# The last 128 tokens of a transformer block's result computed by tokens instead of by channels, with residual and gate brought to that layout by small copies on chip

## The reference, cut to what matters

```
x = x + causal_depthwise_conv(x, cond)          # x: 32 batches x 32 steps x 256 channels
# transformer block, conditioned by cond through six vectors per batch
shift1, scale1, gate1, shift2, scale2, gate2 = split(cond @ ada_w + ada_b, 6)
x1   = ln(x) * (1 + scale1) + shift1
attn = softmax(q k^T / sqrt(128)) v, 16 heads, over the 32 steps of a batch
xa   = x + gate1 * (attn @ out_w + out_b)
x2   = ln(xa) * (1 + scale2) + shift2
h    = gelu(x2 @ ffn_w1 + ffn_b1)               # 1024 hidden values per token
out  = x + xa + gate2 * (h @ ffn_w2 + ffn_b2)   # 1024 tokens x 256 channels
```

## Time and profile before

| | |
|---|---|
| median of 3 runs | 304.48 us (304.09 to 304.7) |
| the profiled execution | 304.34 us, its span 302.5 us |
| TensorE busy | 295.8 us (98% of the span) |
| VectorE busy | 183.0 us (60%) |
| ScalarE, GpSimd busy | 171.4 us (57%), 121.8 us (40%) |
| granted TensorE clock, mean | 0.996 |

### The profile page before, as it was taken

The page is one execution under the profiler, slowest core; times in us unless marked ns, Lnnn a source line. Parts: engine busy times, 40 slices in busy tenths (PEclk is TensorE's granted clock), DMA queues, the critical chain, the costliest instruction groups (busy, mean ns, idle before and its releaser), DMA issues.

```text
span 302.5 us, 6172 instructions
## 1 busy us (share of the span) xinstructions
PE 295.8 (98%) x2598; PEld 250.0 (83%) x2598; DVE 183.0 (60%) x323; ACT 171.4 (57%) x310; POOL 121.8 (40%) x104
## 2 busy tenths in 40 slices
PE   7999999999999999999999999999999999999994
PEld 7896898878898888788888888888888888877884
DVE  3997697997867648472446664350721364859533
ACT  5953377534862765485267736644763695624910
POOL 5207839331811553172337134630916381321410
PEclk9999999999999999999999999999999999999998
DMA  7912422400250061007003400520090000000404
GB/s 227 367 41 71 119 91 70 142 0 2 62 217 0 4 210 71 0 2 277 3 2 111 168 0 2 177 103 0 4 339 8 2 0 3 0 1 2 69 0 69
DMA packets 22427, 23.00 MB, mean 76 GB/s; under 512 B 9240, under 2 KB 15488, under 8 KB 22400
## 3 DMA queue, kind: packets, MB, share of 16 engines
q1 hardware_dynamic: 20720, 22.39, 22.6%
q10 hardware_dynamic: 1680, 0.23, 0.4%
HBM read 21.57 MB, written 1.05 MB: 75 GB/s over the span
## 4 chain that ended last, share of the span: by engine, by line
PE 85%; DVE 11%; POOL 1%; issue 1%; ACT 0%; DVEq 0%; POOLq 0%
PE bank L1051 16%; PE bank L1052 16%; PE bank L1053 16%; PE bank L1139 8%; DVE xc L591 6%; PE bank L1059 5%; PE bank L1061 5%; PE bank L1060 5%; PE bank L1123 3%; PE bank L1267 3%; PE bank L1269 2%; PE bank L1268 2%; DVE pt L741 1%; DVE ol L746 1%; POOL wl L314 1%; PE bank L1010 1%
## 5 line engine op out<-in xcount | busy, mean ns | idle before, releaser
L314 POOL TENSOR_TENSOR wl<-raw,wh 128x512 fp32r<-128x512 f32 x70 | 96.0, 1396 | 119.2 <-ACT wh L387 100.8
L442 ACT ACTIVATE pool<-bank,bT 128x512 f32<-128x512 f32 x56 | 38.5, 688 | 50.4 <-PE bank L1053 50.4
L1051 PE MATMUL bank<-x1h,wl 128*128 128x512 f32 (+1 forms) x180 | 66.8, 371 | 0.0
L1052 PE MATMUL bank<-x1l,wh 128*128 128x512 f32 (+1 forms) x180 | 65.7, 365 | 0.0
L1053 PE MATMUL bank<-x1h,wh 128*128 128x512 f32 (+1 forms) x180 | 65.6, 365 | 0.0
L746 DVE SCALAR_TENSOR_TENSOR ol<-bank,bT,oh 128x512 fp32r<-128x512 f32 x32 | 23.9, 749 | 31.6 <-ACT oh L467 30.8
L591 DVE SCALAR_TENSOR_TENSOR xc<-x,condT,xc 128x496 f32<-128x496 f32 (+27 forms) x76 | 39.9, 593 | 0.1
L387 ACT ACTIVATE wh<-raw 128x512 fp32r<-128x512 f32 x70 | 39.8, 622 | 0.0
L1051 PEld LDWEIGHTS bank<-x1h,wl 128*128 128x128 f32 x180 | 34.0, 189 | 6.4 <-issue 1.0
L1053 PEld LDWEIGHTS bank<-x1h,wh 128*128 128x128 f32 x180 | 34.0, 189 | 5.5
L1052 PEld LDWEIGHTS bank<-x1l,wh 128*128 128x128 f32 x180 | 34.0, 189 | 5.0
(11 more groups left out here) (136 smaller groups left out, 426.0 us busy)
## 6 DMA issues: line engine op xcount, KB each, us to landing
raw<-in_L_cond_qkv_w_dram SPq DMA_DIRECT2D x24, 512.0 KB, 5.7
raw<-in_L_cond_out_w_dram SPq DMA_DIRECT2D x8, 512.0 KB, 3.6
raw<-in_L_cond_ffn_w_dram SPq DMA_DIRECT2D x3, 512.0 KB, 7.0
adaw<-in_L_cond_ada_w_dram SPq DMA_DIRECT2D x1, 1024.0 KB, 10.3
out_dram<-pool SPq DMA_DIRECT2D x12, 64.0 KB, 1.9
xtok<-in_x_dram SPq DMA_DIRECT2D x2, 256.0 KB, 3.1
adaw<-in_L_cond_ada_w_dram SPq DMA_DIRECT2D x1, 512.0 KB, 5.2
xtok<-in_x_dram SPq DMA_DIRECT2D x1, 512.0 KB, 6.0
```

The source lines that it names most:

```text
L314: g.tensor_tensor(wl[:, cols], raw[:, cols], wh[:, cols].bitcast(F32), ALU.subtract)\
L442: a.activation((q_sb if j < GH else k_sb)[:, j % GH, :], src, ACT.Identity, bias=bias(U, j // GH, j % GH)).then_inc(s_ev, 1)
L1051: pe.matmul(dst, wl[:, w_cols], a_hi, start=start, stop=False)
L1052: pe.matmul(dst, wh[:, w_cols], a_lo, start=False, stop=False)
```

## The change: what it does

Half 1 is split at 384 tokens. Pieces 2 and 3 are `ct` 0 and `ct` 1 with the first 384 tokens each, in the old way. The last 128 tokens are computed for both `ct` at once by `ffn2_last`: the hidden values are stationary, the 256 columns of the second layer's weights move, and the result has one token per partition and all 256 channels in a row. It needs no transpose, and it is stored by two DMAs of 64 tokens each (`store_last`), in runs of 1 KB, one from SyncE and one from ScalarE.

Residual and gate are then wanted by tokens too. `last_rest_by_blocks`, put on VectorE between two `hidden_low`, makes gate * bias + residual for the 128 tokens, and transposes it and the gate in blocks of 32 x 32. Sixteen DMAs from SyncE, from one on-chip tile to another, put these blocks where the token layout has them (32 partitions x 4 runs of 128 bytes each). VectorE ends with a multiply by the gate, from the bank, and an add of the rest.

```
-        FFN2_PIECES = [(0, 0, YB[0][:, ALL], ALL), (0, 1, YB[1][:, ALL], ALL), (1, 0, YB[0][:, ALL], ALL),
-                       (1, 1, YB[1][:, FRONT], FRONT), (1, 1, PB[0][:, FRONT], BACK)]
+        ALL, FRONT, BACK = slice(0, HT), slice(0, HT - P), slice(HT - P, HT)
+        FFN2_PIECES = [(0, 0, YB[0][:, ALL], ALL), (0, 1, YB[1][:, ALL], ALL), (1, 0, YB[0][:, FRONT], FRONT),
+                       (1, 1, YB[1][:, FRONT], FRONT)]
...
+        def store_last(eng, i):
+            rows_i = slice(i * P // 2, (i + 1) * P // 2)
+            eng.dma_start(out[B_LAST:B].rearrange("b t c -> (b t) c")[rows_i], last_rows[rows_i]).then_inc(s_out, 16)
...
             # SyncE, after the stores of half 0
+            sp.wait_ge(s_lturn, 2 * CT)
+            for b in range(QB):
+                for i in range(P // T):
+                    sp.dma_start(pe_[T * b:T * (b + 1), :].rearrange("t (q i c) -> t q i c", i=P // T, c=T)[:, :, i, :],
+                                 last_turned[T * i:T * (i + 1), :, T * b:T * (b + 1)]).then_inc(s_lrows, 16)
+            sp.wait_ge(s_turn, 3)
+            for i in range(P // T):
+                store_blocks(sp, 1, 0, i, FRONT)
+            sp.wait_ge(s_turn, 4)
             for i in range(2):
-                store_blocks(sp, 1, 1, i, BACK)
+                store_blocks(sp, 1, 1, i, FRONT)
+            sp.wait_ge(s_fin, 5)
+            store_last(sp, 0)
...
             # ScalarE
             a.wait_ge(s_turn, 4)
-            for i in range(P // T):
+            for i in range(2, P // T):
                 store_blocks(a, 1, 1, i, FRONT)
-            a.wait_ge(s_turn, 5)
-            for i in range(2, P // T):
-                store_blocks(a, 1, 1, i, BACK)
+            a.wait_ge(s_fin, 5)
+            store_last(a, 1)
...
+            def last_rest_by_blocks():
+                v.wait_ge(s_pt, QB * (NU + 1))
+                for ct in range(CT):
+                    rest = by_batch(part(x0, ct, LAST_SPAN))
+                    v.wait_ge(s_lo, CT * (NC + 1) + ct + 1)
+                    v.wait_ge(s_xs, CT + ct + 1)
+                    v.scalar_tensor_tensor(out=rest, in0=ada(GATE2, ct, LAST_SPAN),
+                                           scalar=bT[:, B_F2 + ct:B_F2 + ct + 1],
+                                           in1=by_batch(part(xc, ct, LAST_SPAN)), op0=ALU.mult, op1=ALU.add)\
+                        .then_inc(s_lbias, 1)
+                    v.wait_ge(s_lbias, ct + 1)
+                    v.transpose(by_batch(last_turned[:, ct, :]), rest).then_inc(s_lturn, 1)
+                    v.transpose(by_batch(last_turned[:, CT + ct, :]), ada(GATE2, ct, LAST_SPAN)).then_inc(s_lturn, 1)
...
             hidden_low(1, 5)
+            last_rest_by_blocks()
             hidden_low(1, 7)
...
-            gated(4)
-            turn(4)
+            v.wait_ge(s_f2, 5)
+            v.wait_ge(s_lrows, 16 * QB * P // T)
+            v.tensor_tensor(last_rows, LAST_BANK, last_gate, ALU.mult).then_inc(s_gt, 1)
+            v.wait_ge(s_gt, 5)
+            v.tensor_tensor(last_rows, last_rows, last_rest, ALU.add).then_inc(s_fin, 1)
...
+            def ffn2_last(k):
+                pe.wait_ge(s_hlo[k % 2], (MT + k) // 2 + 1)
+                # w_hi, w_lo: the 256 columns of k's weights
+                pe.matmul(LAST_BANK, hh[:, k, BACK], w_lo, start=(k == 0), stop=False)
+                pe.matmul(LAST_BANK, hl[:, k, BACK], w_hi, start=False, stop=False)
+                m = pe.matmul(LAST_BANK, hh[:, k, BACK], w_hi, start=False, stop=(k == MT - 1))
+                if k == MT - 1:
+                    m.then_inc(s_f2, 1)
```

More of the change, by code:

```diff
@@ L172, in cond_resid_block_kernel @@
         s_turn = sem("result_blocks_turned")
+        s_lbias, s_lturn = sem("last_rest_with_bias"), sem("last_rest_and_gate_turned")
+        s_lrows = sem("last_rest_and_gate_by_tokens")
         s_out = sem("stored")
@@ L211, in cond_resid_block_kernel @@
         ADA_STEPS = [1, 3, 4]
-        ALL, FRONT, BACK = slice(0, HT), slice(0, HT // 2), slice(HT // 2, HT)
-        FFN2_PIECES = [(0, 0, YB[0][:, ALL], ALL), (0, 1, YB[1][:, ALL], ALL), (1, 0, YB[0][:, ALL], ALL),
-                       (1, 1, YB[1][:, FRONT], FRONT), (1, 1, PB[0][:, FRONT], BACK)]
+        ALL, FRONT, BACK = slice(0, HT), slice(0, HT - P), slice(HT - P, HT)
+        FFN2_PIECES = [(0, 0, YB[0][:, ALL], ALL), (0, 1, YB[1][:, ALL], ALL), (1, 0, YB[0][:, FRONT], FRONT),
+                       (1, 1, YB[1][:, FRONT], FRONT)]
+        LAST_BANK = PB[0][:, 0:C]
+        LAST_SPAN = (TOK - P, P)
+        B_LAST = B - QB
+        last_turned = pn[:, :].rearrange("p (q f) -> p q f", q=2 * CT)
+        last_rest, last_gate, last_rows = pe_[:, 0:C], pe_[:, C:2 * C], sd[:, 0:C]
         x_v = x.rearrange("(n q) t c -> (q t) n c", q=QB)
@@ L284, in _ @@
                     sp.dma_start(dst.rearrange("p (k n) -> p k n", k=4), w2_v[:, 0:4, :]).then_inc(s_raw[i], 16)
-            for n, ct in ((0, 0), (0, 1), (1, 0)):
-                sp.wait_ge(s_turn, CT * n + ct + 1)
+            for ct in range(CT):
+                sp.wait_ge(s_turn, ct + 1)
                 for i in range(P // T):
-                    store_blocks(sp, n, ct, i, ALL)
-            sp.wait_ge(s_turn, 5)
+                    store_blocks(sp, 0, ct, i, ALL)
+            sp.wait_ge(s_lturn, 2 * CT)
[7 more added lines that the diff above has]
+            sp.wait_ge(s_turn, 4)
             for i in range(2):
-                store_blocks(sp, 1, 1, i, BACK)
-            sp.wait_ge(s_out, 16 * (5 * P // T))
+                store_blocks(sp, 1, 1, i, FRONT)
+            sp.wait_ge(s_fin, 5)
+            store_last(sp, 0)
+            sp.wait_ge(s_out, 16 * (4 * P // T + 2))
         @block.gpsimd
@@ L1271, in ffn2 @@
                     m.then_inc(s_f2, 1)
+            def ffn2_last(k):
+                pe.wait_ge(s_hlo[k % 2], (MT + k) // 2 + 1)
+                if k < MT // 2:
+                    c0 = 2048 + C * k
+                    w_hi, w_lo = wh[:, c0:c0 + C], wl[:, c0:c0 + C]
+                else:
+                    i, c0 = (k - 4) // 2, C * (k % 2)
+                    w_hi, w_lo = late_hi[:, i, c0:c0 + C], late_lo[:, i, c0:c0 + C]
+                pe.matmul(LAST_BANK, hh[:, k, BACK], w_lo, start=(k == 0), stop=False)
[3 more added lines that the diff above has]
+                    m.then_inc(s_f2, 1)
             last = NU - 1
@@ L1298, in _ @@
             pe.wait_ge(s_gt, CT)
-            for piece in (2, 3, 4):
+            for piece in (2, 3):
                 for k in range(MT):
                     ffn2(piece, k)
+            for k in range(MT):
+                ffn2_last(k)
 _INS = ['x', 'cond_2048', 'L1_cond_ada_w', 'L1_cond_ada_b', 'L1_cond_qkv_w', 'L1_cond_qkv_b', 'L1_cond_out_w',
```

## The result

The changed kernel takes 307.64 us (median of 5, 307.35 to 308.05), the kernel before 304.09 (5 runs, 304.05 to 304.7): ratio 1.0109, 95% interval 1.0097 to 1.0121. It is slower by 1.1%, where "same" was the likeliest, and its time lies above the range of 303.3 to 305.2. The profiled execution took 308.05 us, the longest of the five, its span 306.3.

What follows compares the result with a forecast made beforehand. SyncE's queue was to bound the end: first copy at 289.33 plus 11.04 of steps gives 300.37, plus 1.6 landing 301.97, 0.17 ahead of before; 304.17 profiled, 304.3 against the median, range 303.3 to 305.2; same 0.49.

Steps and rivals of the forecast that it cites:

- the gain at TensorE's end: After TensorE's last product: VectorE done 0.5 us earlier, both last stores issued 0.87 us ahead if nothing else held.
- rival 2: SyncE's queue at the end: all 21 steps take 0.55, last store starts at 301.24, time 305.2 to 305.5; chance 0.17.
- the wait of VectorE for the copies: Before VectorE's last multiply: sixteenth copy lands at most 0.25 us past TensorE's end, and this wait costs nothing.
- signs of being wrong: Gap before SyncE's last store; copy steps over 0.04 from 0.50; L982 after 298.7; TensorE's last product not ending 298.4 within 0.1.
- TensorE's part: TensorE's pieces 2, 3 and last 24 products: 11.30 us against 11.31 before, last product ending at 298.36 as before.
- When the copies can start: VectorE's six operations before the copies: second scalar_tensor_tensor held by GpSimd to about 288.6, SyncE's first copy issued at 289.33.
- What an issue costs: Per DMA on SyncE's queue: 0.50 us for copies, 0.53 for stores of 48 KB; bounds 0.28 and 0.55.
- the 300.37 of the sum: Start of SyncE's last store: first copy at 289.33 plus 22 steps totalling 11.04 us.
- The landing: SyncE's last store, issue to landing: 1.6 us taken, against 1.7 to 1.9 in the rows, landing at 301.97.
- SyncE's store has 1 us of cover: At the end, SyncE's last store waits for its own queue, so 1 us of VectorE's delay by copies stays hidden.
- The threshold in the text: VectorE's wait for the sixteenth copy costs nothing unless copies land later than 2.7 us after their issue.
- -0.17 predicted: End of the kernel: last store lands at 301.97, 0.17 us ahead of 302.14 in the kernel before.

## Why the prediction was wrong, point by point

The mechanism was right in the main: "the gain at TensorE's end is real and is eaten by a queue". The queue was SyncE's, without a break up to the last store but one, and the slower side of it was in the text as rival 2. Its size was wrong, and with it the wait of VectorE for the copies, which the text had at nothing. All four of the text's signs of being wrong came: steps of 0.645, L982 at 301.32, a gap of 0.42 on SyncE's queue ahead of its last store, and a last product that ends at 298.70.

- *TensorE's part* held. From the first product of piece 2 to the start of the last one it took 11.15 us (287.27 to 298.42), against 11.17 before (286.89 to 298.06). That the last product was 0.36 later is no doing of the change: all of this stretch lay 0.4 later in this execution, with the `hidden_low` ahead of the six at 286.14 instead of 285.75, and the lag was there at 26 us.
- *When the copies can start* held in its mechanism, with the second L959 held up by GpSimd as described; that GpSimd's operation decides was shown by the other order of the six and by the same order at an earlier time. That the number came so near, 289.55 against 289.33, is partly luck: the stretch lay 0.4 later, and from the `hidden_low` ahead to the first copy it was 3.41 where the text had 3.58. The working was wrong in one point: transposes of 128 columns did overlap (0.23 and 0.20 from one start to the next), so the second L959 was ready at 287.56 against GpSimd's 287.55, and not 0.2 behind it.
- *What an issue costs* is the step that failed. I took 0.50 for a copy from stores to device memory, with 0.36 for the step behind the first and 0.55 as the upper bound. It was 0.645, with 0.83 behind the first. Fifteen steps from the first copy to the sixteenth took 299.39 - 289.55 = 9.84 instead of 7.36, and the next, to the first store, 0.645 instead of 0.50. That is 2.6 of the 3.25 us by which the last store was later than the 300.37 of the sum. The rest: 0.22 from the start, 0.37 from the open gap, 0.03 in the stores' own steps, which at 0.54 on average were right. Rows 6 and 7 had no DMA that is on chip at both ends, and I counted the number of partitions as the likeness that mattered. The upper bound of 0.55 was one of another kind of DMA, and so none for this kind.
- *The landing* of the last store, 1.6 taken, was 2.2: 0.6 more. I argued that fewer runs take less time; the bounds of 1.7 to 1.9 that the rows gave were too low too. The store of 128 tokens in the same runs of 1 KB landed in 1.7, so it is not the runs; what it is stays open.
- "SyncE's store has 1 us of cover" was wrong in kind: the copies' slower steps delay VectorE and SyncE together, so VectorE's multiply was 2.6 us late, and with SyncE's last store moved away 2.2 us of loss remained. The threshold in the text, a landing later than 2.7 us after issue, looked at the landing (1.83, near enough) and not at the issue.

Together: -0.17 predicted, + 3.25 for the last store's start, + 0.6 for its landing, is 3.7, and the span grew by 3.7 (302.54 to 306.26). Of this, 0.4 is the later stretch of this execution.

The Trainium skill, "DMA: Bandwidth & Descriptors", section "Issuing engines are not separate DMA queues", says that DMAs from several engines save only the time to start them, which is usually small beside the DMA itself. The second part doesn't fit here: one issue of 0.645 is a third of the 1.8 that a copy takes to land, and sixteen in a row took 10 us. The first fits: with a second queue the whole loss of the changed kernel, 3.5 us, was gone.

## What to carry to other kernels

Count DMAs by their issues, and take the price of one from a DMA of the same kind at both ends; where the trace has none, it has no bound either, and the range must say so. Small copies on chip can move a layout for nothing, but only in a stretch where their queue has time: the same sixteen cost 4.0 us (against no copies) when they started at 289.55, and nothing at the program's end when they started 10 us earlier. In a tail, try the whole store as one DMA as well as shared between queues: here one was the better.

## What the runs showed of the hardware

- A DMA between two on-chip tiles took 0.63 to 0.645 us per issue, at 4, 16 and 64 KB and for one run or four per partition; one to device memory 0.475 at 16 KB, 0.50 at 32 KB and 0.53 to 0.56 at 64 KB; a load from device memory 0.49 to 0.51 at 256 and 512 KB. The first copy on an idle queue took 0.75 to 0.78, the first store of 32 partitions 0.32 to 0.38.
- A store of 64 partitions in runs of 1 KB took 0.53 to 0.61 to issue and 2.0 to 2.3 to land, one of 128 partitions 0.36 and 1.7, the first one of 32 partitions on SyncE 0.33, landing in 1.5. The cause is not known.
- A VectorE operation of 128 columns with two on-chip inputs took 1.43 us beside an operation of GpSimd, ending 0.15 behind it, and 0.31 to 0.35 without one; transposes of 128 columns took 0.27 beside it.
- While SyncE issued copies, ScalarE's second store took 0.62 to 0.71 to issue (0.49 with SyncE on stores to device memory, in the kernel without copies). So the queues are not wholly apart.
